# Maxima of two heads at a time, and ternary weights made beside the experts' tiles, in a program of eight layers' halves

## The reference

```python
x = x + L0_xattn(norm(x), ctx, ...)    # attention, 16 heads of 8 channels
x = x + L0_ffn(norm(x), ...)           # 32 experts, top 6
x = x + L1_xattn(norm(x), ctx, ...)    # fp8 attention
x = x + L1_ffn(norm(x), Wr, Wg, Wu, Wd)# 8 experts, top 2
x = x + L2_xattn(norm(x), ctx, ctx)    # attention, 8 heads of 16 channels
x = x + L2_ffn(norm(x), ...)           # ternary weights, 8-bit activations
x = x + L3_xattn(norm(x), ctx, mask)   # masked attention, 16 heads of 8 channels
x = x + L3_ffn(norm(x), w1, w3, w2)    # ternary weights
```

## Time and profile before

| | us |
|---|---|
| median of 3 runs | 2522.51 (2516.19 to 2522.55) |
| the profiled execution | 2525.09 |
| its span, first to last instruction | 2523.3 |
| PE busy in the span | 2034.0 (81%) |
| DVE | 1814.2 (72%) |
| ACT | 1403.7 (56%) |
| POOL | 1186.2 (47%) |

### The profile page before, as it was taken

The page is one execution under the profiler, slowest core; times in us unless marked ns, Lnnn a source line. Parts: engine busy times, 40 slices in busy tenths (PEclk is TensorE's granted clock), DMA queues, the critical chain, the costliest instruction groups (busy, mean ns, idle before and its releaser), DMA issues. The chain is left out here.

```text
span 2523.3 us, 42640 instructions
## 1 busy us (share of the span) xinstructions
PE 2034.0 (81%) x13467; PEld 1242.7 (49%) x13467; DVE 1814.2 (72%) x4020; ACT 1403.7 (56%) x3553; POOL 1186.2 (47%) x1393
## 2 busy tenths in 40 slices
PE   5999698996799999999999849837835437887487
PEld 2444265663567776777777646514412223333144
DVE  4899485665799999999998663368837756888254
ACT  0777422451688888888888713215634423677343
POOL 3444102443788888888887523276312204333100
PEclk9999779998999999999999959958866656899699
DMA  4466313782300000000000042379610025576100
GB/s 133 138 188 171 100 48 106 249 260 82 59 16 20 20 22 16 20 20 22 16 16 3 1 151 88 117 188 237 174 47 1 0 87 133 153 198 159 44 1 34
DMA packets 256886, 223.20 MB, mean 88 GB/s; under 512 B 36441, under 2 KB 237756, under 8 KB 256028
## 3 DMA queue, kind: packets, MB, share of 16 engines
q1 hardware_dynamic: 231932, 173.06, 24.3%
q0 software_dynamic: 12240, 32.39, 5.1%
q10 hardware_dynamic: 12496, 15.03, 1.8%
HBM read 141.98 MB, written 79.32 MB: 88 GB/s over the span
## 5 line engine op out<-in xcount | busy, mean ns | idle before, releaser
L844 ACT ACTIVATE a_PT<-bank 128x512 f32<-128x512 f32 x640 | 355.8, 602 | 148.7 <-PE bank L607 132.3
L734 DVE TENSOR_REDUCE a_nm<-bank 128x2 f32<-128x512 f32 x640 | 409.2, 683 | 35.1 <-PE bank L600 32.9
L600 PE MATMUL bank<-a_stack_k,a_stack_q 48*128 48x256 bf16 (+2 forms) x1280 | 263.2, 298 | 108.9 <-DVE a_nm L734 75.3
L2913 PE MATMUL bank<-f_w,f_zc 128*128 128x512 bf16 x1152 | 283.9, 383 | 22.8 <-DVE f_zc L3021 18.2
L3233 POOL TENSOR_TENSOR f_hr<-f_hr,half_pow 128x4 f32<-128x4 f32 x192 | 244.5, 1273 | 84.8 <-DVE f_hr L3030 84.6
L607 PE MATMUL bank<-a_stack_q,a_stack_k 51*128 51x256 bf16 (+2 forms) x1280 | 252.2, 287 | 8.6 <-ACT a_PT L844 8.0
L600 PEld LDWEIGHTS bank<-a_stack_k,a_stack_q 48*128 48x128 bf16 (+2 forms) x1280 | 91.7, 99 | 272.9 <-DVE a_nm L734 195.8
L3125 ACT ACTIVATE f_Pm<-bank,f_nmax 128x128 f32<-128x128 f32 x512 | 182.5, 382 | 73.5 <-DVE f_nmax L3045 73.5
L622 PE MATMUL bank<-a_PT,a_V 128*32 128x256 f32 x2560 | 188.3, 416 | 1.4 <-ACT a_PT L844 1.4
L2913 PEld LDWEIGHTS bank<-f_w,f_zc 128*128 128x128 bf16 x1152 | 112.2, 99 | 123.0 <-issue 25.4
L3222 POOL TENSOR_TENSOR f_cf<-f_cbr,f_cmr 128x516 f32<-128x516 bf16 x128 | 157.0, 1226 | 12.6 <-DVE f_cb L3070 11.0
(11 more groups left out here) (370 smaller groups left out, 4721.2 us busy)
## 6 DMA issues: line engine op xcount, KB each, us to landing
cut<-a_parts SPq DMA_DIRECT2D x96, 192.0 KB
cut<-a_parts SPq DMA_DIRECT2D x144, 128.0 KB
o<-a_O SPq DMA_DIRECT2D x32, 512.0 KB
a_stack_q<-cut SPq DMA_DIRECT2D x64, 192.0 KB
a_stack_k<-cut SPq DMA_DIRECT2D x64, 192.0 KB
m_w<-in_w SPq DMA_DIRECT2D x32, 368.0 KB
moe_out<-m_oe ACTq DMA_DIRECT2D x32, 256.0 KB
a_num<-o SPq DMA_DIRECT2D x48, 128.0 KB
```

Of the source, the lines that this page charges most:

```text
L600: x = t.matmul(ps[:, n * D:(n + 1) * D], self.stack_q[rows, i, slot, n * P:(n + 1) * P], self.stack_k[rows, i, slot, :], start=True, stop= ...
L734: v.tensor_reduce(self.nm[:, g % 2, :, at % self.J, at // self.J], self.k.bank[h % 3][:, :].rearrange("p (n m) -> p n m", n=2), AX.X, ALU. ...
L844: a.activation(self.PT[:, h % 8, :, :].rearrange("p m n -> p (m n)"), self.k.bank[3 + h % 3][:, :], ACT.Exp).then_inc(self.a_exp.sem, 1)
L2913: x = t.matmul(ps[:, :], self.zc[:, b % 2, j, c_, :], self.fp8.w3[:, m, c_, at:at + BANK], start=(m == 0 and c_ == 0), stop=(m == 2 and c_ ...
```

## The change

It has three parts. In the attentions DVE takes the maxima of two heads with one instruction in each odd step; the scores have banks 0 to 3, in pairs, and the transposed ones banks 4 and 5. The ternary weights of layers 2 and 3 are loaded by SP in `MoeTop2` (in pieces, 15 loads, 6 ahead of the first tile's store and 3 ahead of each of the next three), and DVE does their sums in iterations 4 to 12 (two an iteration, one ahead of `copy_out` and one behind it), PE the totals in iteration 13, and DVE the rounding from iteration 14 on; the attentions have no ternary work left. The gather of batch b + 2 in layer 2's attention is moved from the step `starts(t, 0)` of batch b to its step `starts(t, 15)`, behind parts(b).

```diff
@@ Attention.scores
-            if h >= 3:
-                t.wait_ge(self.v_max.sem, self.v_max.at(h - 2))
+            if h >= 4 and h % 2 == 0:
+                t.wait_ge(self.v_max.sem, self.v_max.at(h // 2 - 1))
-            if w >= 3:
-                t.wait_ge(self.a_exp.sem, self.a_exp.at(w - 2))
+            if w >= 2:
+                t.wait_ge(self.a_exp.sem, self.a_exp.at(w - 1))
-                i, ps = h // self.heads % self.NST, self.k.bank[h % 3]
+                i, ps = h // self.heads % self.NST, self.k.bank[h % 4]
-                if n == 1:
+                if n == 1 and h % 2:
                     x.then_inc(self.p_S.sem, 1)
-                i, ps = w // self.heads % self.NST, self.k.bank[3 + w % 3]
+                i, ps = w // self.heads % self.NST, self.k.bank[4 + w % 2]
@@ Attention.dve
-            if 0 <= t < self.NH:
-                self.maximum(v, t)
+            if 0 <= t < self.NH and t % 2:
+                self.maxima(v, t // 2)
             self.side_vectors(v, t)
...
+    def maxima(self, v, pair):
+        h, J = 2 * pair, self.J
         g, at = divmod(h, 8)
+        v.wait_ge(self.p_S.sem, self.p_S.at(pair + 1))
         if g >= 2 and at == 0:
             v.wait_ge(self.g_nm.sem, self.g_nm.at(g - 1))
+        nm = self.nm[:, g % 2, :, :, at // 2:at // 2 + 1] if J == 2 else self.nm[:, g % 2, :, :, at:at + 2]
+        v.tensor_reduce(nm.rearrange("p n j h -> p (j h) n"), self.k.two_banks(h % 4 // 2).rearrange("p (h n m) -> p h n m", h=2, n=2),
                         AX.X, ALU.max, negate=True).then_inc(self.v_max.sem, 1)
@@ Attention.act
-        if self.ternary:
-            self.ternary.load(a)
@@ Attention.pool
                 if at < self.NV:
                     self.clear_V(g, at)
-                if self.pairs and at + 2 < B:
-                    self.pairs.gather(g, at + 2)
...
                 g.tensor_tensor(self.parts[:, i, :, 2, :], self.rest[:, i, :, :], self.parts[:, i, :, 1, :],
                                 ALU.subtract).then_inc(self.g_p2.sem, 1)
+            at = self.starts(t, 15)
+            if at is not None and self.pairs and at + 2 < B:
+                self.pairs.gather(g, at + 2)
@@ MoeTop2.sp
+        weights = chain.from_iterable(x.loads(sp) for x in self.ternaries)
         for j in range(self.NT):
             r = j % self.RO
+            for _ in range(3 if j else 6):
+                next(weights, None)
             sp.wait_ge(self.v_oe.sem, self.v_oe.at(j + 1))
@@ MoeTop2.pe
         for i in range(self.NT + 3):
+            if i == self.TOTAL + 2:
+                for x in self.ternaries:
+                    t.wait_ge(x.v_mean.sem, x.v_mean.at(1))
+            if i == self.TOTAL:
+                t.wait_ge(self.a_xT.sem, self.a_xT.at(i - 1))
+                for n, x in enumerate(self.ternaries):
+                    x.total(t, self.at_total(n))
@@ MoeTop2.dve
+        sums = chain.from_iterable(x.sums(v) for x in self.ternaries)
+        rounding = chain.from_iterable(x.rounding(v) for x in self.ternaries)
         for i in range(self.NT + 3):
             if 0 <= i - 1 < self.NT:
                 self.product(v, i - 1)
+            if 4 <= i < self.TOTAL:
+                next(sums, None)
+            if i > self.TOTAL:
+                next(rounding, None)
             if i >= 3:
                 self.copy_out(v, i - 3)
             if i == 1:
                 self.places(v)
+            if 4 <= i < self.TOTAL:
+                next(sums, None)
+            if i == self.TOTAL:
+                v.wait_ge(self.p_xT.sem, self.p_xT.at(i + 1))
+                for n, x in enumerate(self.ternaries):
+                    x.means(v, self.at_total(n))
+            if i > self.TOTAL:
+                next(rounding, None)
```

More of the change, by code:

```diff
@@ L1 @@
 from contextlib import ExitStack
+from itertools import chain
 import numpy as np
@@ L102, in __init__ @@
         self.sig = Signals(nc, ctx)
-        self.bank = [ctx.enter_context(nc.psum_tensor(f"bank{i}", [P, BANK], F32)) for i in range(8)]
+        self.psum = ctx.enter_context(nc.psum_tensor("bank", [P, 8 * BANK], F32))
+        self.bank = [self.psum[:, i * BANK:(i + 1) * BANK] for i in range(8)]
         self.X = self.sb("X", [P, B, D])
@@ L261, in total @@
         t.wait_ge(self.v_sum.sem, self.v_sum.at(1))
-        return t.matmul(ps[:, 0:3], self.k.ones[:, :], self.sum[:, :], start=True, stop=True)
+        t.matmul(ps, self.k.ones[:, :], self.sum[:, :], start=True, stop=True).then_inc(self.p_total.sem, 1)
     def means(self, v, ps):
-        return v.tensor_scalar(self.m[:, :], ps[:, 0:3], 1.0 / self.count, self.least, ALU.mult, ALU.max)
+        v.wait_ge(self.p_total.sem, self.p_total.at(1))
+        v.tensor_scalar(self.m[:, :], ps, 1.0 / self.count, self.least, ALU.mult, ALU.max).then_inc(self.v_mean.sem, 1)
     def rounding(self, v):
         c = self.k.dve
+        v.wait_ge(self.v_mean.sem, self.v_mean.at(1))
         c.mark(v.reciprocal(self.inv[:, :], self.m[:, :]))
-        yield
         for j in range(3):
@@ L298, with __init__ @@
     LEAD, TURNED, EXP, VALUES, SUM = 40, 21, 22, 24, 53
-    def __init__(self, k, layer, ternary, pairs=None):
-        self.k, self.layer, self.ternary, self.pairs = k, layer, ternary, pairs
+    def __init__(self, k, layer, pairs=None):
+        self.k, self.layer, self.pairs = k, layer, pairs
         self.hd = hd = 16 if layer == 2 else 8
@@ L352, in side @@
             yield "W", self.ended(t, self.SUM + 2)
-        if self.ternary and t == 60:
-            yield "T", 0
     def order(self):
@@ L641, in side_matmuls @@
         ps = self.side_bank(t, (what, at))
-        if what == "T":
-            self.ternary.total(t, ps).then_inc(self.p_m.sem, 1)
         if what == "N":
@@ L674, in dve @@
         self.dve_parameters(v)
-        sums = self.ternary.sums(v) if self.ternary else iter(())
-        steps = self.ternary.rounding(v) if self.ternary else iter(())
         for t in self.steps():
-            if 0 <= t < self.NH:
-                self.maximum(v, t)
+            if 0 <= t < self.NH and t % 2:
+                self.maxima(v, t // 2)
             self.side_vectors(v, t)
-            if 0 <= t < 60:
-                next(sums, None)
-            if t == 59:
-                for _ in sums:
-                    pass
-            if t == 61 and self.ternary:
-                self.ternary.means(v, self.filled(v, ("T", 0))).then_inc(self.v_m.sem, 1)
-                v.wait_ge(self.v_m.sem, self.v_m.at(self.by_dve["T", 0] + 1))
-            if t > 61:
-                next(steps, None)
-        for _ in steps:
-            pass
     def dve_parameters(self, v):
@@ L1766, with __init__ @@
     RX, RT, RO = 6, 3, Pairs.RO
-    def __init__(self, k, pairs):
-        self.k, self.pairs, self.rows_out = k, pairs, pairs.rows_out
+    TOTAL = 13
+    def __init__(self, k, pairs, ternaries):
+        self.k, self.pairs, self.rows_out, self.ternaries = k, pairs, pairs.rows_out, ternaries
         self.ctx = ExitStack()
@@ L1989, in dve @@
                 self.places(v)
+            if 4 <= i < self.TOTAL:
[6 more added lines that the diff above has]
+                next(rounding, None)
+        for _ in rounding:
+            pass
     def moments(self, v, g):
@@ L3249, in program @@
         if 0 in stages:
-            stage(Attention(k, 0, None))
+            stage(Attention(k, 0))
         if 1 in stages:
@@ L3258, in program @@
         with ExitStack() as memory:
-            pairs = Pairs(k) if 3 in stages else None
-            if 3 in stages:
-                pairs.allocate(memory)
-                stage(MoeTop2(k, pairs))
+            pairs = Pairs(k)
+            l2.allocate(memory)
+            l3.allocate(memory)
+            with ExitStack() as rows:
+                pairs.allocate(rows)
+                if 3 in stages:
+                    stage(MoeTop2(k, pairs, (l2, l3)))
+                if 4 in stages:
+                    stage(Attention(k, 2, pairs))
             if 4 in stages:
-                l2.allocate(memory)
-                stage(Attention(k, 2, l2, pairs))
                 stage(Bitnet(k, l2))
-        if 6 in stages:
-            with ExitStack() as memory:
-                l3.allocate(memory)
-                stage(Attention(k, 3, l3))
+            if 6 in stages:
+                stage(Attention(k, 3))
                 stage(TernaryFfn(k, l3))
```

40 lines of the change are left out of this document (23 added, 17 removed).

## The result

The changed kernel took 2667.24 us (median of 4 runs, 2655.62 to 2676.96), the kernel before 2522.07 beside it. The ratio is 1.0579, 95% interval 1.0534 to 1.0625: by it 146 us more. The forecast was 2572, 50 more, with a range from 2530 to 2612. The kernel became slower as forecast, and in layer 2 by the mechanism that was forecast. Layers 0 and 3 were to give 22 us together and cost 45, so the size was far off.

A forecast was written before the change was run, and what follows sets the result against it. VectorE was taken to set the pace in layers 0 and 3's heads, TensorE in the experts' tiles. Layer 0 -5, tiles +1, layer 2 +71, layer 3 -17 gave +50: 2572 us as a median, range 2530 to 2612.

The forecast's parts named there:

- (d): Layer 2's heads: ten turns of the gather loop, each 11.7 us + L, take 162 us: +58 (41 to 90).
- (e): Layer 2 ahead of the heads: same loop without maxima, first add earlier, batch 5's add later: +18 us (15 to 26).
- (f): Layer 2 behind batch 15's add: no gather left, ten roundings and pairs' savings go: -5 us (-7 to 0).
- L: Layer 2: landing time of a late gather from its second DMA's issue, 4.5 us in the heads, 3.5 ahead of them.
- (a): Attentions: one maximum for two heads saves 0.06 us a pair, 20 us of VectorE; 5 kept in layers 0 and 3 each.
- R3: Rival: two banks for the transposed scores become a bound in layers 0 and 3, +32 instead of -10: 2614; chance 0.12.
- (b): Layer 3: ternary sums and roundings leave the attention, saving 12 us; with (a) layer 3 gives 17 (10 to 24).
- (c): Experts' tiles: both layers' ternary work fits beside them for 1 us, 2 to 4 if that cover fails.
- R1: Rival, layer 2: the gather is in time after all, since parts(b) come earlier with VectorE lighter: 2474; chance 0.07.
- R2: Rival, layer 2: the loop is there but short, L at 2.8, VectorE's savings in full: +17, 2540; chance 0.18.
- R4: Rival, whole kernel: loop and savings cancel within 0.3% (7.6 us); needs R2 and 10 us more; chance 0.03.

The follow-up runs named there:

- m: The changed kernel with a memset of an unused tile on GpSimd ahead of each of layer 2's 14 late gathers; ratio 1.0691.
- k: The kernel before, three banks on each side, with ScalarE's first parts and copies of O cut to 16 columns behind the first batches; ratio 0.9909.
- l: The kernel before with the cut of k and two banks for the transposed scores; ratio 1.0133.
- c: The kernel before with two banks instead of three for the transposed scores, three for the scores; ratio 1.0241.
- d: The kernel before with the first part alone: maxima of two heads at a time, four banks for scores, two for transposed ones; ratio 1.0241.
- e: The kernel before with the ternary move alone, beside the experts' tiles; 2491.54 us, ratio 0.9866.
- j: The kernel before with two banks for the scores and four for the transposed ones; ratio 1.0241.
- f: The kernel before with single maxima, four banks for the scores and two for the transposed ones; ratio 1.0174.
- b: The kernel before with only layer 2's gather of batch b + 2 moved to starts(t, 15); ratio 1.0361.
- p: The kernel before with half of the values' products left out and two banks for the transposed scores; ratio 1.0334.

## Why the prediction was wrong

**The loop (terms (d), (e), (f)): mechanism right, size short.** The gather is behind parts(b), the adds wait for it, and every turn of the loop is there. (d) gave ten turns 162 us; they took 178.4, so +74 for +58, and the term that was too small is the way from the add to the end of the first part. It had 6.9 us in each turn. It took 4.2, 6.0 and 6.1 in the first three turns and 9.1 to 9.2 in the seven behind them, 11 us more in sum, with TensorE at 1.2 GHz behind its idle stretch (as from 1823.28 to 1827.80 in the turn above). From the second issue to the next add it was 4.9 us in the mean where L had 4.5, 4 us more; the issues took 1 us more, and parts were as forecast. The 2 us for the lower clock stood in the text as an end of the range; they belonged in the value (2.2 in each of the seven), since VectorE idle for 5 to 9 us a turn, and TensorE behind it, was part of the forecast itself. (e) had the first add 6.4 us into the stage (6.3 measured) and batch 5's +18 late (+21); L was 4.1 to 5.1 there for 3.5. (f) had -5 behind the last add; it was +0.6: VectorE's savings there bought nothing.

The Trainium skill's rule in the page DMA: Bandwidth & Descriptors, section Anatomy of one DMA — SWDGE (gpsimd) path, of about 2.0 us fixed plus the bytes, would have made L 2.3, an estimate; the least landing after was 2.7, and the second DMA of a batch took 4.9 at the median, and 6.3 in m for the same bytes. The measurements decide: the fixed part alone does not price a gather that other transfers meet.

**Layers 0 and 3 (term (a)): the sign was wrong, and this was R3.** The step that failed: "ScalarE has 12 of 50 us free in both layers, so I keep 5 of the 8 in each (0 to 8)". Free time over 50 us says nothing of a chain that must close in each step. The edit that gives two heads one instruction takes a bank from the other side (61), makes TensorE and VectorE wait for both heads (30), and gets 17 back for the fourth bank and 14 for the width: +61 where the terms had a gain. R3 had the place right and the reason wrong (casts and copies: k and l), and 32 us for layers 0 and 3 together where c shows 23 and 29. The whole change took 45 in layer 0, where TensorE's granted clock was lower too (0.79 in 100:150).

**Layer 3 came out at 0, by cancellation.** Two banks +29 (c), pairs -12 against that (c to d), the ternary work gone -14 to -17 (e; d to after). (b) had 12 for the ternary work, so that term held.

**(c), the tiles: right.** +1.2 with a prediction of +1, and nothing of it above the spread between executions. The page Perfetto Trace Analysis of the Trainium skill, section Matmul Optimizations, asks that all eight PSUM banks be in use. It does not sort these kernels: c leaves one bank unused in the attentions and costs 61 us, but j uses all eight and costs 61 as well, and f, with all eight, costs 44. What the three have in common is a side with two banks.

**The sum.** 61 for the first part, 91 for the gather, -34 for the ternary work are 118; the whole is 146, 28 more with a half interval of some 15. By the profiled executions it lies in two stages. In layer 2 the loop swallows the 17 to 20 us that the ternary work gives. Layer 0 took 346.0 us at a granted clock of 0.88, where the same code took 332.5 at 0.93 in d; the late gather alone left layer 0 at 298.8 and 0.98 (b), so why the clock was lower stays open. Rival R1 (in time) is refuted by the 136.6 us of waiting, R2 (short loop) by ten turns of 178.4 us, and R4 (nothing in sum), which needed R2, with it. The range reached to R3 alone; R3 on top of the loop, which no case of mine was, is what happened: with c's 23 and 29 us in place of my -10 for layers 0 and 3 the sum would have been 2572 + 10 + 52 = 2634. Layer 2 (96 for 71) and layer 0 (45 for 23; d, which adds the pairs' waits, has 31) give 47 more, and layer 3 (0, where 29 less 12 is 17) takes 17: 2664, against 2667 measured.

## What to carry to other kernels

- A DMA issued by an engine that works in order stands behind every wait ahead of it. Before moving one, follow that wait back: if it comes round to the instruction that needs the DMA's data, the move makes a loop, and its length is paid once a turn, whatever else is saved. One step earlier, ahead of the wait, was 98 us cheaper than one step later.
- Buffers between two engines are priced by the chain that they must cover in each step, not by the engine's free share. Going from three banks to two for the transposed scores cost 61 us with 12 of 50 us free on ScalarE, and two for the scores cost as much, with four on the other side; an instruction that serves two heads at once has to earn that and the waiting for the second head.
- Time each part of a change alone: here one of three parts was worth 1.3%, hidden under two that cost 6%.

## What was not expected of the hardware

- Less work for TensorE can cost time. With half of the values left out and two banks (p) the granted clock was 0.50 in layer 3's first heads and the kernel 24 us slower than with all of them (c); with three banks the same cut gained 14 us at a clock of 0.867.
- One maximum over two PSUM banks, 1024 columns, takes 1220 ns, the same as 1024 columns out of SBUF: reading across the bank cost nothing that shows.
- The same indirect DMAs land in 3.7 us at the median or in 5.2, by when they are issued: 1.5 us later in each turn was enough.
